# Moving a layer's key and value projection from a program of its own into the mixture's program

## The reference, cut to what matters

```python
k = (ctx @ Wk.T + bk)        # 1601 x 256, 16 heads of 16; needs nothing of x
v = (ctx @ Wv.T + bv)
x = x + tanh(g_xattn[l]) * attention(layernorm(x), k, v)
# layer 0: 8 experts of 1024, the best 2 of 8 for each token
for e in range(8):
    a, b = split(xf @ w1[e] + b1[e])
    out += gate_e * ((silu(a) * b) @ w2[e] + b2[e])
x = x + tanh(g_ffn[0]) * out
```

## Time and profile before

| what | us |
|---|---|
| median of 3 runs | 1732.86 (1730.92 to 1733.36) |
| the profiled execution, its own time | 1733.47 |
| its span, first to last instruction | 1731.7 |
| mean granted clock of TensorE | 0.915 |
| PE busy in the span | 1477.4 (85%) |
| DVE, ACT, POOL busy | 874.9, 679.4, 364.2 |

### The profile page before, as it was taken

One profiled execution on the slowest core, in us unless ns is written; L12 is line 12 of the kernel. 1 busy time (PEld: TensorE's weight loads), 2 busy tenths in 40 slices (PEclk: granted clock), 3 DMA queues, 4 the chain that ended last, 5 costly groups with the idle time before them and its releaser, 6 DMA issues. The chain is left out here.

```text
span 1731.7 us, 25849 instructions
## 1 busy us (share of the span) xinstructions
PE 1477.4 (85%) x8703; PEld 903.5 (52%) x8704; DVE 874.9 (51%) x2026; ACT 679.4 (39%) x1109; POOL 364.2 (21%) x346
## 2 busy tenths in 40 slices
PE   4678999999998738999999996349999776999993
PEld 2333333333224627999999995212332463666662
DVE  4579898878753542222222223568887354211112
ACT  3223555767684221333333331315778321122221
POOL 0020000199900260000000000020000316034531
PEclk9879999999999768999999998658999877999997
DMA  3720505128224441028503202140100401124434
GB/s 113 244 78 20 181 20 181 40 95 252 83 74 125 171 151 50 23 93 236 138 24 101 96 23 68 57 150 20 36 23 2 134 17 49 32 91 128 148 100 154
DMA packets 110290, 165.44 MB, mean 96 GB/s; under 512 B 16769, under 2 KB 91195, under 8 KB 108031
## 3 DMA queue, kind: packets, MB, share of 16 engines
q1 hardware_dynamic: 78207, 102.63, 19.5%
q0 software_dynamic: 15232, 45.99, 7.8%
q10 hardware_dynamic: 16768, 15.77, 3.0%
HBM read 108.05 MB, written 59.84 MB: 97 GB/s over the span
## 5 line engine op out<-in xcount | busy, mean ns | idle before, releaser
L791 DVE TENSOR_REDUCE mxp<-psA 128x1 f32<-128x384 f32 (+4 forms) x640 | 334.8, 577 | 64.9 <-PE psA L647 45.6
L765 ACT ACTIVATE Pt<-psC 128x1024 f32<-128x1024 f32 (+4 forms) x296 | 256.2, 918 | 156.1 <-PE psC L673 80.8
L647 PE MATMUL psA<-Kst,Qst 97*128 97x384 bf16 (+4 forms) x640 | 182.6, 352 | 34.9 <-DVE mxp L791 18.6
L1443 PE MATMUL psA<-xTt,OT 128*128 128x128 f32 x1728 | 202.4, 278 | 4.2 <-issue 4.1
L1443 PEld LDWEIGHTS psA<-xTt,OT 128*128 128x128 f32 x1728 | 197.5, 193 | 10.4 <-issue 10.4
L791 DVE TENSOR_REDUCE mxpt<-psA 128x1 f32<-128x449 f32 x256 | 145.2, 619 | 34.4 <-PE psA L647 29.4
L673 PE MATMUL psC<-Qst,Kst 100*128 100x512 bf16 (+4 forms) x592 | 151.4, 360 | 0.7 <-ACT Pt L765 0.2
L647 PEld LDWEIGHTS psA<-Kst,Qst 97*128 97x128 bf16 x640 | 55.4, 99 | 179.9 <-DVE mxp L791 130.5
L765 ACT ACTIVATE Ptt<-psC 128x1024 f32<-128x1024 f32 (+1 forms) x128 | 123.8, 1020 | 47.6 <-PE psC L673 47.1
L696 PE MATMUL psO<-Pt,Vaug 128*17 128x512 f32 (+4 forms) x1184 | 141.3, 548 | 0.0
L1534 DVE SCALAR_TENSOR_TENSOR hT<-psA,b,sil 128x128 f32<-128x128 f32 x216 | 64.1, 345 | 152.2 <-ACT sil L1509 152.2
(11 more groups left out here) (292 smaller groups left out, 1997.5 us busy)
## 6 DMA issues: line engine op xcount, KB each, us to landing
rows<-blank SPq DMA_DIRECT2D x4, 4386.0 KB, 18.0
OT<-L_w SPq DMA_DIRECT2D x8, 2048.0 KB
mi<-mask POOLq DMA_DIRECT2D x16, 800.5 KB
Kst<-k_parts SPq DMA_DIRECT2D x12, 800.5 KB, 16.3
w<-L_w SPq DMA_DIRECT2D x8, 1024.0 KB
q_parts<-parts ACTq DMA_DIRECT2D x4, 1536.0 KB, 15.1
Qst<-q_parts SPq DMA_DIRECT2D x48, 128.0 KB, 2.9
Qstt<-q_parts SPq DMA_DIRECT2D x48, 128.0 KB, 2.8
```

Of the source, the lines that this page charges most:

```text
L647: mmi = pe.matmul(out, Qst[0:KA, half[u] % QN, at:at + P], Kst[0:KA, h, k0:k0 + w], start=True, stop=diag is None and not masked)
L765: act.activation(Pt[0:kw, n % SLOTS, :, col:QC], psC[0:kw, n % 2, :].rearrange("p (y t) -> p y t", y=2)[:, :, col:QC], ACT.Exp).then_inc(p ...
L791: dve.tensor_reduce(mxp[:, q, h, pc:pc + 1], psA[:, place_of[("piece", n)] % AB, 0:w], AX.X, ALU.max).then_inc(a_free, 1)
L1443: mmi = pe.matmul(bank(j)[:, i * P:(i + 1) * P], w1[:, side, k, f * P:(f + 1) * P], xTt[:, z, k, :], start=(k == 0), stop=(k == KD - 1))
```

## The change

The separate projection program goes. A new function `second_keys` returns the same work as four pieces of program, and the expert program of each engine begins with its piece. The second half of the scatter goes to the head of POOL's expert program, and ACT, not POOL, now waits for the scatter's landing, between its part of the keys and the loads of the first rows. The five loads of context, weights and biases are issued by SP in the routing program, behind `wr` and ahead of `b1r`, into tiles that live as long as the layer's.

```diff
-        def experts0(xs, ys, tile_e, tile_row, ends, pairs, ws, w_ld, b_ld, key_parts_stored):
+        def second_keys(cT, wk, wv, bk, bvb, c_ld):
+            def sync(sp):
+                for m in range(NJ):
+                    sp.wait_ge(spl, m + 1)
+                    sp.dma_start(Ks[1][:, m * P:(m + 1) * P, :].rearrange("t p s -> p t s"), parts[:, m, :, :])\
+                      .then_inc(stored, 16)
+                sp.wait_ge(stored, 16 * NJ)
+            def scalar(act):
+                act.wait_ge(c_ld, 80)
+                for m in range(NJ):
+                    for c, (a, n) in enumerate(kcols):
+                        act.wait_ge(mm, m * NP + c + 1)
...
+            def tensor(pe):
+                pe.wait_ge(c_ld, 80)
+                for m in range(NJ):
+                    for c, (a, cw) in enumerate(kcols):
+                        if m:
+                            pe.wait_ge(ev, c + 1)
...
+                for j, (k0, kw) in enumerate(key_tiles()):
+                    if j >= 2:
+                        pe.wait_ge(vev, j - 1)
...
+                pe.wait_ge(ev, NJ * NP)
+                pe.wait_ge(vev, NKT)
+            def vector(dve):
...
                     @block.gpsimd
                     def _(pool):
+                        scatter(pool, 1)
                         for z in range(2):
                             pool.sem_inc(yv_free[z], 1)
...
                     @block.sync
                     def _(sp):
-                        key_parts_stored(sp)
+                        keys_sync(sp)
...
                     @block.tensor
                     def _(pe):
+                        keys_tensor(pe)
                         pe.sem_inc(y, 2)
                         pe.wait_ge(b_ld, 32)
...
+                        keys_scalar(act)
+                        scattered(act)
                         for z in range(2):
                             load_rows(slice(z, z + 1), z)
...
                     @block.vector
                     def _(dve):
+                        keys_vector(dve)
                         dve.sem_inc(hd, NJ)
...
                 def loads(sp, ot, n):
+                    sp.dma_start(cT[:, :, :], ctxT_d.rearrange("(k p) s -> p k s", p=P)).then_inc(c_ld, 16)
+                    sp.dma_start(wk[:, :, :], W[1]["WkT"].rearrange("(k p) n -> p k n", p=P)).then_inc(c_ld, 16)
+                    with nc.allow_non_contiguous_dma(reason="bias columns"):
+                        sp.dma_start(bk[:, :], W[1]["bk"].rearrange("(m p) -> p m", p=P)).then_inc(c_ld, 16)
+                    sp.dma_start(wv[:, :, :], W[1]["WvT"].rearrange("(k p) n -> p k n", p=P)).then_inc(c_ld, 16)
+                    sp.dma_start(bvb[:, :], W[1]["bv"].rearrange("(a n) -> a n", a=1).to_broadcast([P, D])).then_inc(c_ld, 16)
                     sp.dma_start(b1r[:, :], F["b1"].rearrange("e (f p) -> (e f) p", p=P)).then_inc(b_ld, 16)
...
-                def rows_to_experts(pool):
-                    scatter(pool, 1)
-                    scattered(pool)
-
-                key_parts_stored = projections("c", None, 1, beside=rows_to_experts)
-                experts0(xs0, ys0, tile_e, tile_row, ends, pairs, (w1, w2, b1r, b2), w_ld, b_ld, key_parts_stored)
+                keys = second_keys(cT, wk, wv, bk, bvb, c_ld)
+                experts0(xs0, ys0, tile_e, tile_row, ends, pairs, (w1, w2, b1r, b2), w_ld, b_ld, keys,
+                         scatter, scattered)
```

More of the change, by code:

```diff
@@ L1356, in load_expert @@
                             F["w2"][e].rearrange("(k p) n -> p k n", p=P)).then_inc(w_ld, 16)
-        def experts0(xs, ys, tile_e, tile_row, ends, pairs, ws, w_ld, b_ld, key_parts_stored):
+        def second_keys(cT, wk, wv, bk, bvb, c_ld):
+            NJ = KD
+            room = Kst[:, :, :].rearrange("p h s -> p (h s)")
+            n_parts = NJ * 3 * S
+            parts = room[:, 0:n_parts].rearrange("p (b t s) -> p b t s", b=NJ, t=3)
+            full = room[:, n_parts:n_parts + 2 * NJ * S].bitcast(F32).rearrange("p (b s) -> p b s", b=NJ)
+            kcols = groups_of(S, 512)
+            NP = len(kcols)
+            mm, ev, spl, stored = (sem(f"k1_{n}") for n in ("done", "evacuated", "split", "stored"))
+            chain, vmm, vev = (sem(f"k1_{n}") for n in ("chain", "v_done", "v_evacuated"))
+            def sync(sp):
[8 more added lines that the diff above has]
+                    for c, (a, n) in enumerate(kcols):
+                        src = bank(c)[:, 0:n]
+                        act.wait_ge(mm, m * NP + c + 1)
+                        act.activation(full[:, m, a:a + n], src, ACT.Identity, bias=bk[:, m:m + 1], scale=1.0)
+                        act.activation(parts[:, m, 0, a:a + n], src, ACT.Identity, bias=bk[:, m:m + 1], scale=1.0)\
+                           .then_inc(ev, 1)
+            def tensor(pe):
[4 more added lines that the diff above has]
+                            pe.wait_ge(ev, c + 1)
+                        for k in range(KD):
+                            mmi = pe.matmul(bank(c)[:, 0:cw], wk[:, k, m * P:(m + 1) * P], cT[:, k, a:a + cw],
+                                            start=(k == 0), stop=(k == KD - 1))
+                        mmi.then_inc(mm, 1)
+                for j, (k0, kw) in enumerate(key_tiles()):
+                    if j >= 2:
+                        pe.wait_ge(vev, j - 1)
+                    for k in range(KD):
+                        mmi = pe.matmul(bank(6 + j % 2)[0:kw, 0:D], cT[:, k, k0:k0 + kw], wv[:, k, :],
+                                        start=(k == 0), stop=(k == KD - 1))
+                    mmi.then_inc(vmm, 1)
+                pe.wait_ge(ev, NJ * NP)
+                pe.wait_ge(vev, NKT)
+            def vector(dve):
+                dve.wait_ge(c_ld, 80)
+                for m in range(NJ):
+                    f, (p0, p1, p2) = full[:, m, :], (parts[:, m, t, :] for t in range(3))
+                    dve.wait_ge(ev, (m + 1) * NP)
+                    dve.tensor_tensor(f, f, p0, ALU.subtract).then_inc(chain, 1)
+                    dve.wait_ge(chain, 3 * m + 1)
+                    dve.tensor_copy(p1, f).then_inc(chain, 1)
+                    dve.wait_ge(chain, 3 * m + 2)
+                    dve.tensor_tensor(p2, f, p1, ALU.subtract).then_inc(chain, 1)
+                    dve.wait_ge(chain, 3 * m + 3)
+                    dve.sem_inc(spl, 1)
+                for j, (k0, kw) in enumerate(key_tiles()):
+                    dve.wait_ge(vmm, j + 1)
+                    dve.tensor_tensor(Vaug[0:kw, j, :, 0:DH], bank(6 + j % 2)[0:kw, 0:D].rearrange("p (h d) -> p h d", h=H),
+                                      bvb[0:kw, :].rearrange("p (h d) -> p h d", h=H), ALU.add).then_inc(vev, 1)
+            return sync, scalar, tensor, vector
@@ L1362, in experts0 @@
+        def experts0(xs, ys, tile_e, tile_row, ends, pairs, ws, w_ld, b_ld, keys, scatter, scattered):
             w1, w2, b1r, b2 = ws
@@ L1385, in pair_count @@
                     return eng.value_load(pairs[0:1, 0:1], min_val=1, max_val=NT0 // 2)
+                keys_sync, keys_scalar, keys_tensor, keys_vector = keys
                 with nc.Block() as block:
@@ L1863, in ffn_layer @@
                 w_ld, b_ld = sem("e0_weights"), sem("e0_biases_loaded")
+                cT = sb(st, "cT1", [P, KD, S])
+                wk, wv = sb(st, "wk1", [P, KD, D]), sb(st, "wv1", [P, KD, D])
+                bk, bvb = sb(st, "bk1", [P, KD]), sb(st, "bvb1", [P, D])
+                c_ld = sem("k1_loaded")
                 def loads(sp, ot, n):
+                    sp.dma_start(cT[:, :, :], ctxT_d.rearrange("(k p) s -> p k s", p=P)).then_inc(c_ld, 16)
[4 more added lines that the diff above has]
+                    sp.dma_start(bvb[:, :], W[1]["bv"].rearrange("(a n) -> a n", a=1).to_broadcast([P, D])).then_inc(c_ld, 16)
                     sp.dma_start(b1r[:, :], F["b1"].rearrange("e (f p) -> (e f) p", p=P)).then_inc(b_ld, 16)
```

## The result

| | before | after |
|---|---|---|
| median of 5 runs, us | 1732.86 (1730.29 to 1735.45) | 1721.99 (1719.10 to 1724.22) |
| the profiled execution's own time | 1733.47 | 1720.29 |
| its span | 1731.7 | 1718.6 |
| mean granted clock | 0.915 | 0.918 |

The ratio of the runs is 0.9924, with a 95% interval of 0.9897 to 0.9951: faster by 8.5 to 17.8 us. The medians differ by 10.9. The forecast was 9.4 saved, 1723.5, with a range of 1719.8 to 1728.5: the median lies inside, the ratio's middle (0.9924 x 1732.86 = 1719.7) just outside, on the fast side. So by these runs somewhat more came than was forecast.

A forecast was written before the change was run, and what follows sets the result against it. TensorE was taken to wait for input-only loads, then run a key and value chain before the expert loop. With the scatter ending last, 9.4 us saved from the 1732.86 median gave 1723.5 us, range 1719.8 to 1728.5.

The forecast's parts named there:

- The place and the cause: At the separate projection program's opening, TensorE waits for input-only loads; issuing them earlier moves the key chain by 8.8 us.
- Scatter ends last: Before the expert loop, the scatter, not the key chain, ends last by about 2 us; 9.4 us saved, chance 0.62.
- the scatter's end: GpSimd's scatter, with the splits in its middle, is stretched by 6.0 us and ends at 650.5.
- the floor: Least stretch of GpSimd's scatter by the splits: 4.9 us as before, end at 649.4.
- the ceiling: Every microsecond of split stops GpSimd's scatter, 9.3 us, end at 653.8; as a rival 6.1 saved, 1726.8, chance 0.10.
- the landing: From the scatter's last instruction to ACT's first row load: 3.24 us, so rows issued at 653.8, 9.4 us earlier.
- The unchanged 32.5 us: The chain of keys, splits and values, to the last V addition's end, keeps its 32.5 us and ends at 653.2.
- From there to the loop nothing changes: From ACT's first row load to the first up matmul stays 7.98 us, so the loop starts at 661.8.
- A shift of the loop's start goes through whole: The expert loop keeps TensorE busy 44.00 of 44 us, so nothing in it can take up an earlier start.
- slower rival: The expert loop loses its instruction supply; 4.11 us in each of 17 later passes would give 1793, chance 0.04.

The follow-up runs named there:

- only the merge: Changed kernel, but the five loads are issued at the head of the merged program, not in the routing program: 1729.04 us, ratio 0.9972 to the kernel before.
- no splits: Changed kernel with VectorE's six split instructions replaced by four memsets, the keys' second and third parts zero: 1717.82 us, ratio 0.9905 to the kernel before.
- three row DMAs: Changed kernel with the first three indirect DMAs of the scatter's second half issued in the routing program: 1721.82 us, ratio 0.9930 to the kernel before.
- second measurement: The changed kernel run again, unaltered, against the kernel before on the same chip: 1722.41 us against 1734.05, ratio 0.9928.
- both kernels with the long gap: Changed kernel with values ahead of keys and key stores behind the first rows, 1724.75 us; the same plus three early row DMAs, 1719.12 us.

## Why the prediction was right or wrong

**The place and the cause were right.** The first key matmul moved to the opening (0.02 us behind it), the early loads cost the routing program nothing that can be told (77.1 us from `wo`'s load to the last table in one profile and 80.4 in the other, 79.1 and 79.2 before), and `wo`'s first matmul came 7.3 us behind its load. The part that did most is the early loads, 9.6 us at the loop's start by themselves; the merge by itself gave 3.2, and both together 12.25.

**Scatter ends last: right.** Forecast by 2 us over the chain, measured by 1.2. Three kernels held by the chain (only the merge, no splits, three row DMAs) put the first up matmul 5.46 to 5.49 us behind b1r, the changed kernel 6.69.

**The failed step is its first, the scatter's end.** I laid the splits over GpSimd's instructions and got a stretch of 6.0 us; without the splits the scatter is 4.0 shorter, less than the 4.9 taken as the floor from the kernel before. The pattern itself was as described (632.75 + 2.29 is 0.84 behind the end of the split at 632.37 + 1.83), but fewer instructions were caught than I laid out: a DMA of 1.73 us and one of 2.29, a label copy of 1.49 and a DMA of 1.53, 3.9 us over their undisturbed 0.98, 0.98, 0.20 and 0.98. The scatter's end came 2.0 us ahead of the forecast (27.81 against 29.8), most of the 2.8 that the loop came earlier.

By the Trainium skill's "GPSIMD Engine Reference", section "Specifications", VectorE instructions with two SBUF inputs contend with GpSimd: the run without them agrees in kind, and the V additions, one input of which is in PSUM, did not contend. The page gives no price; the ceiling of 9.3 us that the prediction took for that rule is far from the 4.0 measured.

**The second mis-sized term is the landing.** I took 3.24 us between the last scatter instruction and the dependent issue from the second layer's routing, and 2.54 came, 0.7 less. In the runs it was 4.08 and 5.25 us beside the stores of key parts and 2.5 to 2.7 without them. The row it was taken from doesn't hold by itself either. In the changed kernel the same load of the second layer was issued only 1.58 us behind the same scatter (1460.72 - 1459.14):

```profile
1458.16 0.98 POOL L875 DMA_INDIRECT rows<-fxn,slot  x1 [0.31 <-issue]
...
1460.72 0.37 SPq L1679 DMA_DIRECT2D OT<-rows  x1
```

Over all profiles that distance lies between 1.49 and 3.28 us, 3.24 and 3.23 in the two of the kernel before. What sets it is not shown.

**The unchanged 32.5 us** were 31.5: the first twelve key matmuls took 5.80 us against 6.48. This hid under the scatter.

**"From there to the loop nothing changes"** held: 7.98 us forecast, 7.93 measured. **"A shift of the loop's start goes through whole" did not:** 3 us went again, 1.0 in the first 48 up matmuls at the lower clock, 1.4 at GpSimd's exit and 0.6 in places not found. My slower rival had looked for instruction supply within the loop, where it cost nothing (43.9 to 44.0 us busy of 44 in each window); the exit behind the loop was not thought of. The section "Instruction fetch mechanics" of the Trainium skill's "Runtime: NRT & Kernel Launch" speaks of a fetch where a branch leaves what is held; that the exit's 5.55 to 7.20 us and the entry's 4.1 to 7.3 us are such fetches is not shown. The traces do list transfers of the kind "instruction", and none begins within the gaps of 6.97 and 7.27 us or within the exit's 6.91 us; the one nearest to the loop's start begins 0.5 us behind the first up matmul in both kernels with the long gap. The register reads at the loop's entry are an untested rival.

So two errors stood against each other: the loop starts 2.8 us earlier than forecast and its program ends 3 us later than a plain shift, 9.3 us net from the opening to the next program. That this is close to the forecast's 9.4 is luck. The timed runs show 10.9 and 11.6; the interval of the second measurement, 9.5 to 15.4 us, just misses 9.3. What makes the last 1.5 to 2 us is not settled; 0.6 of it could lie in the routing program (a mean of 78.6 us against 79.2), and the untouched programs differ by more than that from execution to execution.

## What to carry to other kernels

When a wait on loads is taken from a chain, size what was hidden behind that chain as a path of its own, from its last instruction through its landing to the first reader: here it took over by 1.2 us. Large stores that nobody needs yet belong neither beside a landing on the path (1.5 us and more) nor beside a loop's entry (3 us); give them a wait on something late. And before an effect is read from one pair of profiles, profile the kernel before twice: 3.5 us of the difference here lay in a program nobody had touched.

## What the runs showed of the hardware that was not expected

- The next block opened 0.5 us behind VectorE's last instruction, but 2.7 us behind an indirect DMA of GpSimd that ended at the same time. With one early row DMA it was 2.8, with three 2.7 and 2.8.
- TensorE's entry into the loop took 4.1 to 4.8 us without large transfers, and 7.0 and 7.3 us with 2.4 MB of stores in flight. The indirect DMA's landing grew from 2.5 to 2.7 us to 4.1 and 5.2 beside such stores.
- GpSimd's exit from its program: 5.55 to 5.58 us (separate program), 6.66 to 6.92 (merged), 7.20 (96 idle increments more).
- TensorE's granted clock falls at different points of the two routing programs in executions of the same kernel: the same 16 matmuls took 5.49 us at 0.67 and 3.72 at 1.00. The second layer's routing took 117.3 and 113.8 us in two profiles of the kernel before, 112.1 and 112.2 in two of the changed one.
